# Quantised 3x3 convolution on one core: from a mix of direct and Winograd bands to five products per pair of rows, with the low product scaled inside PSUM

## What is computed

```python
mask   = _predictor_mask(x)                  # 8x8 block means >= 0.05, spread back over the block
x_high = jnp.where(mask, x, EPS)
x_low  = jnp.where(mask, EPS, x)
y_high = _conv(_quant_act_uint(x_high, act_scale_high, 8), _quant_weight_per_oc(w_high, 8))
y_low  = _conv(_quant_act_uint(x_low,  act_scale_low,  4), _quant_weight_per_oc(w_low,  4))
return y_high + y_low                        # (32, 128, 56, 56)
```

## Time and profile before

| | before |
|---|---|
| median of three runs | 687.96 us |
| the profiled execution's span, first to last instruction | 685.9 us |
| busy: PE / DVE / ACT / POOL | 94% / 97% / 80% / 44% |
| matmuls of 128x448 | 3264, 102 per image |
| DVE instructions | 902 |
| DMA | 104 MB, mean 152 GB/s |
| chain that ended last | PE 85%, DVE 6%, ACT 4% |

### The profile page before, as it was taken

How to read it: one execution, slowest core, us unless ns; L and a number is a source line. 1 busy time by engine, 2 the same in 40 slices (tenths; PEclk the granted TensorE clock), 3 DMA queues, 4 the chain that set the end, 5 groups by cost and what they waited for, 6 DMA issues and landing times.

```text
span 685.9 us, 11103 instructions
## 1 busy us (share of the span) xinstructions
PE 647.6 (94%) x3312; PEld 315.9 (46%) x3312; DVE 663.5 (97%) x902; ACT 550.4 (80%) x616; POOL 301.3 (44%) x240
## 2 busy tenths in 40 slices
PE   0489999999999999999999999999999999999998
PEld 0234444444444444444444444444444444444443
DVE  6999999999999999999999999999999999999984
ACT  5588898888898888888888889888889888888843
POOL 5943433553443554353454343355334345434343
PEclk9999999999999999999999999999999999999999
DMA  6222244533344443334443334443333444333223
GB/s 256 94 96 107 122 189 187 187 147 129 125 161 187 187 165 141 122 134 187 187 187 146 115 123 179 187 187 150 136 127 148 187 187 176 141 111 134 95 95 148
DMA packets 14842, 104.07 MB, mean 152 GB/s; under 512 B 1904, under 2 KB 2160, under 8 KB 10864
## 3 DMA queue, kind: packets, MB, share of 16 engines
q1 hardware_dynamic: 14832, 103.95, 39.6%
HBM read 52.56 MB, written 51.38 MB: 152 GB/s over the span
## 4 chain that ended last, share of the span: by engine, by line
PE 85%; DVE 6%; ACT 4%; issue 3%; DMA 1%; DVEq 0%; SPq 0%
PE psum L440 85%; DVE ybuf L678 3%; ACT parts L550 3%; ACT rounded_h L463 1%; DMA act_scale_l<-act_scale_low 1%; DVE pooled L588 0%; DVE chosen L598 0%; DVE v_h L224 0%; DVE clipped_l L604 0%; ACT rounded_l L463 0%; DVE w_max_h L576 0%; DVE plane_h L613 0%; DVE w_max_l L576 0%; ACT wint_l L500 0%; ACT mask_l L481 0%
## 5 line engine op out<-in xcount | busy, mean ns | idle before, releaser
L234 POOL TENSOR_TENSOR sums<-parts 128x448 f32<-128x448 f32 x126 | 140.6, 1136 | 364.4 <-DVE ybuf L678 364.4
L440 PE MATMUL psum<-v_h,wT_h 128*128 128x448 f16 x768 | 192.4, 358 | 9.4 <-DVE ybuf L678 9.3
L440 PE MATMUL psum<-v_l,wT_l 128*128 128x448 f16 x768 | 192.1, 358 | 1.1 <-POOL v_l L228 1.1
L440 PE MATMUL psum<-plane_h,wT_h 128*128 128x448 f16 x864 | 184.4, 358 | 0.0
L440 PE MATMUL psum<-plane_l,wT_l 128*128 128x448 f16 x864 | 182.8, 356 | 0.0
L588 DVE TENSOR_REDUCE pooled<-xbuf 128x7 f32<-128x448 f32 (+1 forms) x213 | 134.6, 632 | 0.0
L238 POOL TENSOR_TENSOR ybuf<-parts,sums 128x896 f32<-128x896 f32 x63 | 131.9, 2094 | 4.9
L678 DVE SCALAR_TENSOR_TENSOR parts<-psum,out_scale_l,parts 128x448 f32<-128x448 f32 x192 | 129.2, 674 | 3.3 <-ACT parts L550 3.2
L440 PEld LDWEIGHTS psum<-plane_h,wT_h 128*128 128x128 f16 x864 | 83.2, 97 | 85.7 <-DVE parts L678 6.3
L440 PEld LDWEIGHTS psum<-plane_l,wT_l 128*128 128x128 f16 x864 | 83.5, 97 | 84.2 <-issue 0.4
L440 PEld LDWEIGHTS psum<-v_h,wT_h 128*128 128x128 f16 x768 | 71.6, 97 | 93.4 <-DVE ybuf L678 23.2
(11 more groups left out here) (73 smaller groups left out, 360.4 us busy)
## 6 DMA issues: line engine op xcount, KB each, us to landing
xbuf<-x SPq DMA_DIRECT2D x31, 1568.0 KB, 7.5
y<-ybuf SPq DMA_DIRECT2D x31, 896.0 KB, 3.9
y<-ybuf SPq DMA_DIRECT2D x32, 672.0 KB, 3.0
xbuf<-x SPq DMA_DIRECT2D x1, 896.0 KB, 8.4
xbuf<-x SPq DMA_DIRECT2D x1, 672.0 KB, 9.6
wraw_h<-w_high SPq DMA_DIRECT2D x1, 576.0 KB, 5.7
wraw_l<-w_low SPq DMA_DIRECT2D x1, 576.0 KB, 6.7
y<-ybuf SPq DMA_DIRECT2D x2, 224.0 KB, 2.7
```

The source lines that it names most:

```text
L234: ops.tensor_tensor(sums[w][:, e, :], parts[w][:, PART_AT[1], :], parts[w][:, PART_AT[2], :], op).then_inc(summed, 1)
L440: last = nc.tensor.matmul(psum[:, 2 * pair + (k == "l"), 0:N], stationary(k, j, t), moving(k, p, row, j, t), start=(t == 0), stop=(t == co ...
```

## The change

All 56 rows are now computed in one way. A pair of output rows (2t, 2t + 1) is made of three sums: T, which both rows share, is the middle row of weights applied to the sum of plane rows 2t + 1 and 2t + 2; A and B are the rest of the even and of the odd row. With g0, g1, g2 the three rows of weights, A = g0 * row(2t) + (g2 - g1) * row(2t + 2) and B = (g0 - g1) * row(2t + 1) + g2 * row(2t + 3), up to the constant offsets. That makes five products (fifteen matmuls) per path. A band has seven pairs, so 392 columns, and there are four bands: 4 x 2 x 15 = 120 matmuls per image.

- The inputs of T are `rowsum` (rows one `PITCH` apart); A and B read the plane itself, two `PITCH` apart. `transform`, `merge`, `parts`, `sums` and all of POOL's work after the start are gone.
- Two sets of three PSUM banks (A, B, T) take turns. The low product of a band is written first; ACT multiplies all three banks in place by `ratio` = low scale / high scale (`low_scaled`); then the high product is added on it in the same banks. ACT takes T out with scale and bias into `shared` (`shared_tile`), and DVE makes each output row as A or B times the scale plus `shared` (`out_row`).
- PE's order per image: low 0, low 1, high 0, high 1, low 2, low 3, high 2, high 3.
- The high path's clip goes to DVE (`clip`), and clips, masks, averages and row sums of every image come in two parts, of 32 and 24 rows. The averages are two DVE instructions instead of seven, and they, `choose`, masks and the rest belong to image n + 1 instead of n + 1 and n + 2.
- Start: image 0 is prepared in the two parts, the first before the high weights; the low weights and the first part of x are loaded first, the two scales through ACT's queue; the weights are combined on DVE. Stores are two halves of 28 rows, for the last image too.

```diff
+            def products(k, p, band, tile):
+                out = psum[:, BANK[band % 2][tile], 0:N]
+                parts = [(row, mat + dx, dx) for row, mat in PRODUCTS[tile] for dx in range(3)]
+                for j, (row, mat, dx) in enumerate(parts):
+                    last = nc.tensor.matmul(out, wT[k][:, mat, :], moving(k, p, band, row, dx),
+                                            start=(k == "l" and j == 0), stop=(j == len(parts) - 1), ...)
+            def low(n, p, band):
+                if band % 2 == 0:
+                    pe.wait_ge(s_rowsum["l"], 2 * n + band // 2 + 1)
+                if new:
+                    pe.wait_ge(s_shared, g - 1)
+                products("l", p, band, "T")
+                if new:
+                    pe.wait_ge(s_out, 2 * g - 3)
+                products("l", p, band, "A")
+                if new:
+                    pe.wait_ge(s_out, 2 * g - 2)
+                products("l", p, band, "B").then_inc(s_low, 1)
+            def high(n, p, band):
+                if band % 2 == 0:
+                    pe.wait_ge(s_rowsum["h"], 2 * n + band // 2 + 1)
+                pe.wait_ge(s_scaled, g + 1)
+                for tile in "TAB":
+                    products("h", p, band, tile).then_inc(s_high, 1)
```

```diff
+            def moving(k, p, band, row, dx):
+                if row is None:
+                    return rows(rowsum[k][p], band * T_ROWS * PITCH + 1 + dx, PITCH, T_ROWS)
+                return rows(plane[k][p], (2 * band * T_ROWS + row) * PITCH + 1 + dx, 2 * PITCH, T_ROWS)
```

ACT for image n (q is the part; `after` and the first image's lines left out):

```diff
+                quantise("l", *ahead, 0)
+                low_scaled(n, 0)
+                quantise("l", *ahead, 1)
+                low_scaled(n, 1)
+                shared_tile(n, 0)
+                quantise("h", *ahead, 0)
+                shared_tile(n, 1)
+                quantise("h", *ahead, 1)
+                low_scaled(n, 2)
+                act.wait_ge(s_chosen, n + 3)
+                masks(n + 1, 0, BY)
+                low_scaled(n, 3)
+                shared_tile(n, 2)
+                shared_tile(n, 3)
```

DVE for image n, with m = n + 1:

```diff
+                pool_part(mi, mp, 0); pool_part(mi, mp, 1); choose(m, 0, BY, 2 * m + 2)
+                clip("l", m, 0); clip("l", m, 1)
+                out_row(n, p, 0, 0); out_row(n, p, 0, 1)
+                clip("h", m, 0)
+                out_row(n, p, 1, 0); out_row(n, p, 1, 1)
+                apply_mask("l", m, mp, 0); clip("h", m, 1); apply_mask("l", m, mp, 1)
+                row_sums("l", m, mp, 0); apply_mask("h", m, mp, 0); row_sums("l", m, mp, 1)
+                out_row(n, p, 2, 0); out_row(n, p, 2, 1)
+                apply_mask("h", m, mp, 1)
+                out_row(n, p, 3, 0)
+                row_sums("h", m, mp, 0)
+                out_row(n, p, 3, 1)
+                row_sums("h", m, mp, 1)
```

More of the change, by code:

```diff
@@ L38, in conv_program @@
     P = 128
-    assert C == P and OC == P and H == 56 and W % POOL == 0 and B % 2 == 0 and B >= 6
+    assert C == P and OC == P and H == 56 and W == 56 and B % 2 == 0 and B >= 6
     BY, BX = H // POOL, W // POOL
     HW = H * W
-    ROWS = POOL
-    N = ROWS * W
-    assert N <= 512
     PITCH = W + 2
     PLANE = (H + 2) * PITCH + 4
[L47 to L60, removed]
+    PAIRS = H // 2
+    BANDS = 4
+    T_ROWS = PAIRS // BANDS
+    N = T_ROWS * W
+    assert N <= 512
+    SUMS = PAIRS * PITCH + 2
+    CUT = (0, 4, BY)
+    PART = [(CUT[q], CUT[q + 1]) for q in range(2)]
+    MATS = TAPS + 6
+    G21, G01 = TAPS, TAPS + 3
+    BORDERS = 8
+    TILES = 3
     xd = x.rearrange("b c h w -> b c (h w)")
@@ L84, in conv_program @@
         mask = {k: sb(f"mask_{k}", [P, BY, W], F16) for k in "hl"}
[L86 to L88 removed]
+        shared = [sb(f"shared{s}", [P, N], F32) for s in range(2)]
         wraw = {k: sb(f"wraw_{k}", [P, TAPS, C], F32) for k in "hl"}
@@ L146, in conv_program @@
-        s_last_merged = sem("last_band_merged")
+        s_shared = sem("shared_ready")
+        s_out = sem("y_rows_ready")
         s_stored = [sem(f"y_stored{p}") for p in range(2)]
         block = ctx.enter_context(nc.Block())
[L150 to L161, removed]
@@ new lines, in store, with step @@
+                sp.dma_start(yd[bass.ds(n, 1), :, part * half:(part + 1) * half].rearrange("b c n -> (b c) n"),
+                             ybuf[p][:, part * half:(part + 1) * half]).then_inc(s_stored[p], 16)
+            load_after(0, 0)
+            def step(i, p, load=True):
+                store(i, p, 0)
+                if load:
+                    load_after(i + p, 1 - p)
+                store(i, p, 1)
+            step(0, 0)
+            step(0, 1)
+            with sp.Fori(1, B // 2 - 2) as i:
@@ new lines, in body @@
+                if early(n):
+                    pe.wait_ge(s_border[p], BORDERS)
+                for pair in range(BANDS // 2):
+                    if first_image(n) and pair == 0:
+                        pe.wait_ge(s_wT["l"], 2)
+                        low(n, p, 0)
+                        turn_weights("h")
+                        sum_weights("l")
+                        sum_weights("h")
+                        low(n, p, 1)
+                    else:
+                        low(n, p, 2 * pair)
+                        low(n, p, 2 * pair + 1)
+                    high(n, p, 2 * pair)
+                    high(n, p, 2 * pair + 1)
@@ new lines, in _ @@
+            act_scales()
+            weights("l")
+            pool_part(0, 0, 0)
+            choose(0, *PART[0], 1)
+            clip("l", 0, 0)
+            apply_mask("l", 0, 0, 0)
+            row_sums("l", 0, 0, 0)
+            weights("h")
+            clip("h", 0, 0)
+            apply_mask("h", 0, 0, 0)
+            row_sums("h", 0, 0, 0)
+            low_ratio()
+            pool_part(0, 0, 1)
+            choose(0, *PART[1], 2)
+            for k in "lh":
+                clip(k, 0, 1)
@@ new lines, in body @@
+                if not early(n):
+                    dve.wait_ge(s_stored[p], 32 * i)
+                out_row(n, p, 0, 0)
+                out_row(n, p, 0, 1)
+                if after:
+                    clip("h", m, 0)
+                out_row(n, p, 1, 0)
+                out_row(n, p, 1, 1)
+                if after:
+                    apply_mask("l", m, mp, 0)
+                    clip("h", m, 1)
+                    apply_mask("l", m, mp, 1)
+                    row_sums("l", m, mp, 0)
+                    apply_mask("h", m, mp, 0)
+                    row_sums("l", m, mp, 1)
```

544 lines of the change are left out of this document (209 added, 335 removed).

## The result

The changed kernel takes 698.36 us (median, 698.33 to 698.41) against 687.87 us for the kernel before, a ratio of 1.0153 with a 95% interval of 1.0139 to 1.0167. The forecast was 699.1 us.

The account below looks back on a forecast made before the run. DVE bounded the kernel before, PE's matmuls would bound the changed one: start 26.0 + 32 x 20.83 = 692.6, plus 0.25 + 0.6 + 0.1 + 3.5 = 697.0 span, plus 2.06 to the median, 699.1 us; range 691 to 709.

Parts of the forecast that it names:

- The pace before: Kernel before, per image: DVE sets the pace by a little at 20.33 us; PE would set it at 19.9.
- The matmul term, +16.0 us: PE's 120 matmuls per image: 20.83 us against 20.33, so +0.50 x 32, if PE is never kept waiting.
- per row: Matmul step taken as proportional to rows read, 7 of 56 for 8 of 56: T 0.170 us, A and B 0.1746.
- fixed: Bound on the matmul step: all excess over 2.4 GHz a fixed cost of a matmul, an image then 20.97 us.
- The reading surcharge: Matmuls reading every second row cost more, 0.1995 against 0.194 us before; 96 of 120 now read so, before 24 of 102.
- The rival that it costs little at 392 columns: A and B matmuls: reading every second row costs little, not slower; 9% for an image of 20.5 us or less.
- PE is not kept waiting: Mid-run, `low_scaled` of some 1.25 us fits in 2.6; the tightest chain, over the masks, leaves 1.1 us to spare.
- The bound of three separate operations, 1.9: ACT's `low_scaled`: 1.9 us if the three banks took three separate operations, against some 1.25 expected.
- The rival of the ACT and DVE chain: Masks behind low 2 and a scaling take PE's place: 0.6 us an image late, 718 us; chance 14%, mostly 702 to 718.
- The start, -6.3 us: Before the images: first image virtually begins at 26.0 us against 32.3; bounds 23 and 29.
- The 0.4 for slow matmuls: Start, image 0: 0.4 us added for slow matmuls after PE's pause, moving the virtual beginning from 25.6 to 26.0.
- The end, +0.8 us: After the last matmul: DVE needs 0.6 us, then a 784 KB store 3.5; bounds +0.3 and +1.5.

Follow-up runs that it names:

- Experiment 7: Kernel before with `choose` moved from DVE to GpSimd for images 2 to 31, plus a tiny addition ahead of it: 675.34 us, 0.982.
- experiment 8: Kernel before with PE's inputs (`plane`, `v03`, `v1`, `v2`) laid one element (2 bytes) further: 689.64 us, 1.0026.
- experiment 2: Changed kernel with planes and row sums laid one element (2 bytes) further in SBUF: 691.1 us, 1.0059 of the kernel before.
- experiment 1: Changed kernel with A and B reading rows that follow each other, so wrong rows and no convolution: 687.3 us, 0.999 of the kernel before.
- experiment 5: Changed kernel with a second ACT pass, factor 1, over bank T alone behind each in-place scaling: 699.99 us.
- experiment 4: Changed kernel with a second ACT pass, factor 1, over all three banks behind each in-place scaling: 764.4 us, 1.111.
- Experiment 6: Changed kernel with the two scales loaded first on SyncE's queue instead of on ACT's queue: 695.56 us.
- experiment 3: Changed kernel with ACT's masks for the next image made ahead of `low_scaled(n, 2)` instead of behind it: 699.36 us.
- experiment 10: Changed kernel with planes and row sums one element further and the scales first on SyncE's queue: 687.47 us, 0.9998 of the kernel before.

## Why the prediction was right, point by point

- **The pace before** (PE 19.9, DVE at 20.33): right. Experiment 7 took DVE's load away and an image fell to 19.89; experiment 8 took 0.2 us of PE's load away and the time didn't fall.
- **The matmul term, +16.0 us**: right in kind, a little large: 20.76 us an image for 20.83, +13.8. T stepped at 0.170 as said, A and B at 0.174 for 0.1746. For the excess over 2.4 GHz, 13 ns at eight rows became 11 at seven, as "per row" has it; but these are averages over taps of quite different cost (experiment 2), mixed in other shares than before, so the choice between "per row" and "fixed" isn't settled by them.
- **The reading surcharge** is where the loss is: experiment 1 without it is level with the kernel before. The rival that it costs little at 392 columns fell, but its reason, that the price hangs on where a row begins, was half of the truth: by the table of experiment 2 every second row costs nothing at one beginning and 10 ns at another. The prediction took one price for all and met the average. The step by the Trainium skill (TensorE: Matmul & The Clock Gate, "Back-to-back issue gap"), 165.8 ns, is met by the best taps (165); T's three average 170 and the twelve of A and B 174, so here it is about the floor and not the step.
- **PE is not kept waiting**: right in the changed kernel, PE busy 540 of 540 us. `low_scaled` took 1.22 us (stated 1.25, bounds 1.2 to 1.9), `choose` 0.19, DVE stood 3.8 us ahead of the masks and was busy 75% of the span, where about 80% was said. But the margin was wrong. "It would cost from 2.3 us on" held each scaling against its own 2.4 us and forgot ACT's queue between the two of a pair: 1.8 us is still free (experiment 5, 0.15 us to spare), 2.45 costs 2.06 us an image (experiment 4). The bound of three separate operations, 1.9, would have been at the edge, not well inside. The rival of the ACT and DVE chain was priced at 0.6 us an image for a scaling of 2.4; experiment 4 shows 2.06. It had its chance for too cheap a price.
- **The start, -6.3 us**: -4.5. The failed step is "the scales are used at 7.4 as now" (DVE's first weights instruction then): ACT's queue did issue them from 0.75, but beside the large loads the second took 8.2 us to land and DVE began at 9.39, 3.4 late. Experiment 6 gives 2.8 us of it back. A part of the delay was made up by rounding of the weights on DVE in 0.87 us, where 1.3 was put down.
- **PE's stand in image 0**: said "some 3 us before high 0"; the wait was 3.05 us. The 0.4 for slow matmuls behind it was not needed in the profiled execution, where T and A after it ran at the full step; in experiments 3, 5, 6 and 10 a pause of 3.0 to 3.6 us was followed by matmuls at half the clock, which cost 1.4 to 1.5 us. That the start came no later than this is luck that the forecast had not reckoned with.
- **The end, +0.8 us**: +1.2 from the issue of the last store, inside the bounds.

So the errors of the start (gain 1.8 too high), of the end (0.4 too little) and of the matmuls (2.2 too much) cancelled. What is left of the 0.7 us between forecast and result are small things: the 0.6 by which the sum over the whole span was rough, and a step from span to median of 1.8 us where 2.06 was taken. That the number is so near is luck; the mechanism, PE alone at the step of its reading pattern, is what the runs bear out.

## What to carry to other kernels

An engine's columns are not its time: when a change replaces contiguous reads by reads of every second row, take the step of a group that already reads that way, not the average, and multiply; and look at each tap by itself, since here the same pattern stepped at 165 or at 176 ns by where its rows began. Taking work off the engine that paces a kernel brings only the distance to the next one, here 0.44 of 1.2 us, so work out that distance first. And test a wait against the whole queue that stands ahead of it, over as many rounds as buffers allow, not against its own operation.

## What was unexpected of the hardware

- The step of a matmul with fp16 inputs depends on where the rows begin, together with their distance: at 392 columns in rows of 56, 232 bytes apart, 165, 173 or 176 ns (table of experiment 2), all at full granted clock. In experiment 2 a shift of 2 bytes for all of PE's inputs took 0.26 us off an image of 20.76, 1.3%, with nothing else changed; DVE's masks into the same shifted buffers kept their time (1.10 us against 1.09).
- Two transfers of 0.5 KB on a second queue, issued at 0.75 and 1.19 us beside loads of 576 to 1568 KB, landed after 5.9 and 8.2 us; issued ahead of those loads on the same queue they were used 3.4 us sooner.
- ACT's pass over three PSUM banks in one instruction, 1176 elements from PSUM to PSUM, took 1.22 us, where the 448 elements of the earlier trace rows took 0.62.
- Behind a pause of PE of 3.0 us the granted clock fell to 0.50 in some executions and stayed at full in another, in the same place of nearly the same program (experiment 6); it cost 1.4 to 1.5 us each time.
